# Attention stage: square roots of two batches in a row, three distance buffers, scores two batches ahead

## The reference

```python
P = einsum('btd,ed->bte', Xn, W_in) + b_in      # q, k, v and a gate for each head
sq = q2 + swapaxes(k2, -1, -2) - 2.0 * einsum('bhqd,bhkd->bhqk', Q, K)
dist = sqrt(maximum(sq, 0.0))
W = (1e-4 + dist) ** -2
W = W / (1e-4 + sum(W, axis=-1, keepdims=True))
A = einsum('bhqk,bhkd->bhqd', W, V)
return X + einsum('btd,ed->bte', (G * A) as rows, W_out) + b_out
```

## Time and profile before

| | |
|---|---|
| time, median of 3 runs | 1530.92 us (1530.58 to 1532.08) |
| profiled execution: its time / its span | 1532.71 / 1531.0 us |
| busy of the span: PE, DVE, ACT, POOL | 1312.3, 1277.3, 1095.3, 900.0 us |
| mean granted clock of TensorE | 0.888 |
| attention stage: first distance to last Exp | 832.5 to 1237.3 us |

### The profile page before, as it was taken

One profiled execution on the slowest core, in us unless ns is written; L12 is line 12 of the kernel. 1 busy time (PEld: TensorE's weight loads), 2 busy tenths in 40 slices (PEclk: granted clock), 3 DMA queues, 4 the chain that ended last, 5 costly groups with the idle time before them and its releaser, 6 DMA issues. The chain is left out here.

```text
span 1531.0 us, 21357 instructions
## 1 busy us (share of the span) xinstructions
PE 1312.3 (86%) x6384; PEld 631.9 (41%) x6384; DVE 1277.3 (83%) x2166; ACT 1095.3 (72%) x1578; POOL 900.0 (59%) x1054
## 2 busy tenths in 40 slices
PE   4688888888887699999997788878788669999998
PEld 3344444444443244444443233333333334444443
DVE  2799999999999978788886788888888558888885
ACT  4677777777777446666653899999999956656664
POOL 4988888989887746566665332322222016656665
PEclk8899999999999899999998677676766679999999
DMA  7113112211211022333220000000000023323331
GB/s 249 56 56 111 55 55 64 101 56 55 96 70 56 0 112 112 151 152 139 110 111 1 1 1 0 0 0 0 0 0 0 1 111 119 119 117 118 141 154 64
DMA packets 27923, 111.54 MB, mean 73 GB/s; under 512 B 4049, under 2 KB 9570, under 8 KB 19426
## 3 DMA queue, kind: packets, MB, share of 16 engines
q1 hardware_dynamic: 27010, 110.21, 19.2%
q10 hardware_dynamic: 864, 0.74, 0.2%
HBM read 108.06 MB, written 2.88 MB: 72 GB/s over the span
## 5 line engine op out<-in xcount | busy, mean ns | idle before, releaser
L1042 POOL TENSOR_TENSOR e_h_lo<-e_h,e_h_hi 128x512 f16<-128x512 f32 x272 | 314.9, 1159 | 247.6 <-ACT e_h_hi L1124 235.1
L275 POOL TENSOR_TENSOR m_h<-m_b_sb,m_dx 128x512 f32<-128x512 f32 x256 | 345.7, 1377 | 51.6 <-POOLq L67 40.1
L521 ACT ACTIVATE m_decay<-m_delta,mw_a_log 128x255 f32<-128x255 f32 x448 | 185.3, 461 | 117.3 <-DVEq L695 117.1
L690 DVE TENSOR_TENSOR_SCAN m_h<-m_decay,m_h 128x1024 f32<-128x1024 f32 x112 | 255.9, 2285 | 13.5 <-DVEq L60 7.7
L391 PE MATMUL m_y_ps<-m_hc,ident 128*128 128x512 f32 x512 | 260.7, 635 | 0.0
L1119 ACT ACTIVATE e_g<-e_g 128x512 f32<-128x512 f32 x256 | 148.9, 582 | 126.0 <-PE e_g L1064 124.3
L1124 ACT ACTIVATE e_h_hi<-e_h 128x512 f16<-128x512 f32 x272 | 169.8, 624 | 82.4 <-DVE e_h L1175 80.3
L1621 DVE TENSOR_SCALAR a_d<-a_s 128x512 f32<-128x512 f32 x256 | 170.4, 687 | 55.6 <-PE a_s L1508 35.9
L1064 PE MATMUL e_g<-ef_x_hi,ew_gate_up 128*128 128x512 f16 x544 | 207.9, 382 | 3.8 <-PEq L103 2.4
L1069 PE MATMUL e_y<-e_h_hi,ew_down 128*128 128x512 f16 x544 | 205.9, 379 | 2.4 <-POOL e_h_lo L1042 2.4
L1064 PE MATMUL e_u<-ef_x_hi,ew_gate_up 128*128 128x512 f16 x544 | 207.9, 382 | 0.0
(11 more groups left out here) (234 smaller groups left out, 2067.1 us busy)
## 6 DMA issues: line engine op xcount, KB each, us to landing
e_c_rest<-mix SPq DMA_DIRECT2D x48, 1024.0 KB, 8.7
m_b_sb<-b_rows SPq DMA_DIRECT2D x64, 512.0 KB, 5.4
ef_c_head<-mix SPq DMA_DIRECT2D x16, 1024.0 KB, 4.6
ew_gate_up<-w_gate_up SPq DMA_DIRECT2D x1, 2176.0 KB, 13.5
out<-x_sb SPq DMA_DIRECT2D x8, 256.0 KB, 2.3
ew_down<-w_down SPq DMA_DIRECT2D x1, 1088.0 KB, 11.7
mw_conv_rows<-w_conv_rows ACTq DMA_DIRECT2D x1, 640.0 KB
mix<-ef_cT SPq DMA_DIRECT2D x16, 32.0 KB, 1.6
```

What stands on the lines that cost most here:

```text
L275: ins = nc.gpsimd.tensor_tensor(h[:, m % 4, :, c], b_sb[:, p, 2 * m:2 * m + 2], dx[:, p, c:c + 1].to_broadcast([P, 2, T]), ALU.mult)
L521: ins = nc.scalar.activation(decay_of(m, p)[:, at + 1:at + T], delta[:, p, c, 1:T], ACT.Exp, scale=neg_a[:, c, 2 * m + n:2 * m + n + 1])
L690: nc.vector.tensor_tensor_scan(flat, decay_of(m, p)[:], flat, 0.0, ALU.mult, ALU.add).then_inc(scan_chain, 1)
L1042: nc.gpsimd.tensor_tensor(h_lo[:, k], h[:, k], h_hi[:, k], ALU.subtract).then_inc(h_lo_ready, 1)
```

## The change

ScalarE no longer alternates between the two tables for each batch. It takes the square roots of batches 1 and 2 in a row, then Ln and Exp of batch 1 and of batch 2, and so on for 3 and 4 up to 13 and 14; batches 0 and 15 are done alone as before. For that the scores run two batches ahead (LEAD = 2): body b makes the distances of batch b+2 and the front of batch b+3, into three buffers in turn. The run of bodies begins with b = -2, and six bodies form a loop. The table load for Ln now waits for the roots by a semaphore of its own.

Steps change their places as well. VectorE: the statistics go from head 14 to ahead of distance 0, `normalise` from head 0 to 3, `read_zT` from 4 to 6, the wait for the kept gate from 7 to 9, `read_qkvg` from 8 to 9, `split_qk` from 12 to 13, `update` from 13 to 14. TensorE: `transpose_z` from head 1 to 5. POOL: the norm from the end of a body to its head. The statistics of batch 1, which the expert stage ahead made, move to body -2.

```diff
--- before.py
+++ after.py
@@ AttentionFront.vector_step
         if e == 8:
             self.read_qkvg(dve, 0, banks)
-        if e == 9:
-            self.statistics(dve, 1)
...
@@ attention_layer
         WEIGH_AT = (13, 14, 15)
+        D_BUFS, LEAD, TURN = 3, 2, 6
...
-        d = sb("d", [P, 2, NH, TT * T])
+        d = sb("d", [P, D_BUFS, NH, TT * T])
...
-        def batches(eng, body, prologue, epilogue):
-            prologue()
-            body(-1, 1, core=False, tail=False)
-            body(0, 0, tail=False)
-            with eng.Fori(0, NB // 2 - 2) as i:
-                body(i * 2 + 1, 1)
-                body(i * 2 + 2, 0)
-            body(NB - 3, 1, further=False)
-            body(NB - 2, 0, further=False, ahead=False)
-            body(NB - 1, 1, further=False, ahead=False, heads=False, last=True)
+        def batches(eng, body, epilogue):
+            def run(b, n):
+                body(b, n % 2, n % D_BUFS, n % 2 == 1, opening=n == -LEAD, core=n >= 0, tail=n >= 1, keeps=-1 <= n < NB - 1,
+                     heads=n < NB - LEAD, ahead=n < NB - LEAD - 1, single=n in (0, NB - 1), last=n == NB - 1)
+
+            for n in range(-LEAD, 1):
+                run(n, n)
+            with eng.Fori(0, (NB - LEAD - 2) // TURN) as i:
+                for n in range(1, TURN + 1):
+                    run(i * TURN + n, n)
+            for n in range(NB - LEAD - 1, NB):
+                run(n, n)
             epilogue()
...
@@ POOL, body
-                if ahead:
-                    front.residual(pool, b + 2)
+                if ahead:
+                    front.norm(pool)
+                    front.residual(pool, b + LEAD + 1)
                 if tail:
                     take(pool, gate_free)
-                if heads:
+                if keeps:
                     keep(1 - p)
                 if ahead:
-                    front.pack(pool, p)
-                if further:
-                    front.norm(pool)
+                    front.pack(pool, 1 - p)
...
@@ TensorE, body
-                        score(h, 1 - p, not core)
+                        score(h, p, opening)
                     if h == 1 and tail:
                         weights.wait(-1)
-                        weigh(HG - 1, 1 - p)
-                    if h == 1 and ahead:
-                        front.transpose_z(pe, t_ps[0])
+                        weigh(HG - 1, 1 - p, (k - 1) % D_BUFS)
                     if h == 4 and tail:
                         transpose_av()
+                    if h == 5 and ahead:
+                        front.transpose_z(pe, t_ps[0])
                     if h == 8 and ahead:
                         front.project(pe, t_ps)
...
@@ ScalarE, body
+                def root(buffer):
+                    for first, n in ((0, 8), (8, 4), (12, 4)):
+                        take(act, d_ready)
+                        nc.scalar.activation(heads_of(buffer, first, n), heads_of(buffer, first, n), ACT.Sqrt).then_inc(root_chain, 1)
...
-                for first, n in ((0, 8), (8, 4), (12, 4)):
-                    take(act, d_ready)
-                    nc.scalar.activation(heads_of(first, n), heads_of(first, n), ACT.Sqrt).then_inc(act_chain, 1)
-                nc.scalar.preload_act_table_set("natural_log_exp_and_others")
+                if single or paired:
+                    root(k)
+                    if not single:
+                        root((k + 1) % D_BUFS)
+                    act.wait_ge(root_chain, 3 if single else 6)
+                    act.sem_inc(root_chain, -3 if single else -6)
+                    nc.scalar.preload_act_table_set("natural_log_exp_and_others")
                 for half in range(2):
-                    act.wait_ge(act_chain, 1 + 2 * half)
...
@@ VectorE, body
                 for h in range(NH):
+                    if h == 0 and ahead:
+                        front.statistics(dve, b + LEAD + 1)
                     if heads:
-                        distance(h, 1 - p)
-                    if h == 0 and ahead:
-                        front.normalise(dve, b + 2)
+                        distance(h, (k + LEAD) % D_BUFS)
...
-                    if h == 4 and ahead:
+                    if h == 3 and ahead:
+                        front.normalise(dve, b + LEAD + 1)
+                    if h == 6 and ahead:
                         front.read_zT(dve, t_ps[0])
                     if h == 6 and tail:
                         norm_and_gate(1 - p)
-                    if h == 7 and core:
+                    if h == 9 and keeps:
                         take(dve, gate_ready)
-                    if h == 8 and ahead:
-                        front.read_qkvg(dve, p, t_ps)
+                    if h == 9 and ahead:
+                        front.read_qkvg(dve, 1 - p, t_ps)
                     if h == 10 and tail:
                         read_oT()
-                    if h == 12 and ahead:
-                        front.split_qk(dve, p)
-                    if h == 13 and tail:
+                    if h == 13 and ahead:
+                        front.split_qk(dve, 1 - p)
+                    if h == 14 and tail:
                         update(b - 1)
-                    if h == 14 and further:
-                        front.statistics(dve, b + 3)
...
                     if h == 15 and ahead:
-                        front.read_qkT(dve, p, t_ps)
+                        front.read_qkT(dve, 1 - p, t_ps)
```

More of the change, by code:

```diff
@@ L1477, in keep, with body @@
                 nc.gpsimd.tensor_scalar(gate[:, p], qkvg[:, p, :, 3 * W:4 * W], 1.0, 1.0, ALU.mult, ALU.mult).then_inc(gate_ready, 1)
-            def prologue():
-                front.norm(pool)
-            def body(b, p, core=True, tail=True, heads=True, ahead=True, further=True, last=False):
+            def body(b, p, k, paired, opening, core, tail, keeps, heads, ahead, single, last):
                 if last:
@@ L1572, in body @@
                             weights.wait(g, not tail)
-                            weigh(g, p)
+                            weigh(g, p, k)
                 if heads:
-                    scores_read.end(not core, False)
+                    scores_read.end(opening, False)
                 if core:
-                    weights.end(not tail, not heads)
+                    weights.end(not tail, last)
             def epilogue():
                 weights.wait(HG - 1)
-                weigh(HG - 1, 1)
+                weigh(HG - 1, (NB - 1) % 2, (NB - 1) % D_BUFS)
                 transpose_av()
@@ L1674, in body @@
                         read_av(0)
-                    if h == 2 and tail:
                         read_av(1)
-                    if h == 4 and ahead:
+                    if h == 3 and ahead:
+                        front.normalise(dve, b + LEAD + 1)
+                    if h == 6 and ahead:
                         front.read_zT(dve, t_ps[0])
@@ L1708, in epilogue @@
                 update(NB - 1)
-            batches(dve, body, lambda: None, epilogue)
+            batches(dve, body, epilogue)
 def program(nc, x, w, out, mix, b_rows):
```

31 lines of the change are left out of this document (15 added, 16 removed).

## The result

The changed kernel takes 1554.16 us (median of 4 runs, 1552.46 to 1558.92) against 1531.47 (1530.58 to 1532.08): 1.0154 times the time before, 95% interval 1.0129 to 1.0179. It is slower by 22.7 us, where +12 was forecast. Its runs scatter by 6 us, those of before by 1.5.

The account below looks back on a forecast made before the run. The VectorE and TensorE loop was to replace ScalarE as bound: a start of 901.5, 11 bodies of 24.4 and the tail put the last Exp 12.1 us later, 1530.9 + 12.1 = 1543 us; range 1525 to 1551, forecast's own 1535 to 1548.

Parts of the forecast that it names:

- What bounds: Attention stage: ScalarE bounds at 24.36 us a batch; the VectorE and TensorE loop, about 23.1, is next, about 1.2 behind.
- Part 1, the loads: ScalarE's table loads: 14 fewer, worth 18 us; with a 0.15 wait a pair takes 46.1, a batch 23.05.
- Part 2, the start: First bodies: ScalarE waits for batch 2's distances before batch 1's Ln; batch 2 ends 10.9 us later.
- Part 3 (b): VectorE, end of distance 6 to start of distance 10: readings no longer cover the projection; 6.05 becomes 7.65, +1.6 us.
- Rival 1: ScalarE stays the bound, bodies at or under 23.05 us, about 22 with the projection at full clock; 1525 us; chance 0.17.
- F: Length of a body in the attention stage, forecast at 24.4 us; the difference in time is 11 x F - 256.3.
- Part 3 (a) and (c): Body's start to the end of distance 6, -0.15 us; and from distance 10 on, -0.56 or +0.15.
- (c): Rest of the body from distance 10, 10.3 us before: -0.56 if VectorE is late there, +0.15 if score 15 is late.
- two sums: Body lengths worked out step by step from bodies 1 and 2 of before: 23.9 and 24.9 us, middle 24.4.
- Part 4, the end: From body 12's start at 1169.9 through the last pair and batch 15 alone: last Exp at 1249.4, +12.1 us.
- Rival 3: TensorE's longer waits keep weighing and qk transposes at half clock; bodies 25.0 to 25.3, +19 to +22, 1551 us; chance 0.14.

Follow-up runs that it names:

- e1: Changed kernel with the kept-gate wait and the readings of q, k, v, g put back ahead of distance 9 (head 8); 1529.39 us, ratio 0.9977.
- e2: Kernel before, with only the readings of q, k, v, g moved from behind distance 8 to behind distance 9; 1547.26 us, ratio 1.0107.
- e13: e1 with every batch done singly on ScalarE, 32 table loads; 1529.35 us, ratio 0.9990.
- e11: Changed kernel with two extra unused matmuls of 256 columns behind each of scores 2, 3, 5, 6 and 7; 1533.33 us, ratio 1.0017.
- e4: Changed kernel with every batch done singly on ScalarE, 32 table loads; 1548.09 us, ratio 1.0108.
- e7: Changed kernel with six extra unused matmuls of 256 columns behind score 10; 1548.08 us, ratio 1.0117.
- e14: e7 with its bodies written out instead of looped; 1544.85 us, ratio 1.0097.
- e8: e1 with two extra unused matmuls of 256 columns behind each of scores 2, 3, 5, 6 and 7; 1529.07 us, ratio 0.9988.
- e5: Changed kernel with its bodies written out instead of looped; 1541.74 us, ratio 1.0072.
- e9: e1 with its bodies written out instead of looped; 1525.35 us, ratio 0.9964.
- e10: e8 with its bodies written out and two extra unused matmuls behind scores 10 and 11 as well; 1533.41 us, ratio 1.0006.
- e3: Changed kernel's pairs, three buffers and lead of two, with every step at its head of before and bodies written out; 1536.38 us, ratio 1.0032.

## Why the prediction was right and wrong

The direction, and the mechanism that carries it, were right. Step by step:

- **What bounds.** Right. A batch on ScalarE takes longer than the loop of VectorE and TensorE, and with the change that loop took its place as the bound. e1, e2 and e13 show it: with ScalarE bound or nearly so, 1529; with the loop at 25.4 or more, 1547 and more, pairs or no pairs. But the lead was 24.36 - 23.57 = 0.8 us over the first five bodies, not 1.2.
- **Part 1, the loads.** Right: 18 in the stage, the wait ahead of the load 0.10 (0.15 was taken), and a pair takes 46.1 (e1, from the load at 927.16 to that at 975.42, less a wait of 2.20). In the looped kernels the net worth is nothing that can be told from zero (e13 against e1), since what they win is lost at the start and to the loop. The Trainium skill counts 2.66 us a switch ("ScalarE: Activation LUTs", What ACT_TABLE_LOAD costs); the rows do not agree, a switch costs 1.29 to 1.30 in them.
- **Part 2, the start.** Too dear by 3: body 1 starts at 898.05, not 901.5; the cost is 7.8, not 10.9. The three bodies took 21.6, 22.0 and 22.9 (22.7, 22.7 and 23.5 were taken): the wait for score 9 came in them too, 2.4 to 3.0 us, but most other waits of the first bodies of before went.
- **Part 3 (b).** Right: stretch (2) was to be 7.65 - 0.35 = 7.3 and is 7.18, and distance 9 waits 1.57 (1.55). That this wait hangs on the projection at half clock is shown by e11. Rival 1 had put F at about 22 for that case; it is 23.48 there, since (3) is 10.6.
- **Part 3 (a) and (c), the step that failed.** The length of a body, F, was put at 24.4 and is 25.41. In the stretches of the table the prediction's two sums are on average 7.2 + 7.3 + 9.9 = 24.4; the trace has 7.49 + 7.18 + 10.73. Two terms were too small. The first is the model: bodies 1 and 2 of before, 23.0 and 23.3 us, are the two shortest; the first five average 23.57, because in two of them (3 and 5) the transposes of av run at half clock and (1) is 8.0 instead of 6.9. That is 0.4 us. The second is (c), the rest of the body behind distance 10: it was taken as shorter by 0.56 or longer by 0.15, so 0.2 shorter on average, and it is 0.6 longer than in the first five bodies of before (10.73 against 10.15). That is 0.8 us, and it comes with more of the weighing and of the transposes of q and k at half clock, as bodies 9 and 10 show. The other two stretches give 0.2 back. Over 11 bodies the 1.01 us are +11.1 us; body 1 starts 3.4 earlier than forecast, and the tail is 0.3 longer: 12.1 + 8.0 = 20.1, what the last Exp shows.
- **Part 4, the end.** Right: body 12 starts at 1177.57 and the last Exp ends 79.85 later; 79.5 was worked out. e4 shows that this tail is a price of pairs by itself, about one batch of Ln and Exp (14.5 us).
- **Range.** Its upper end, 1551, was too low by 3 us for the median of 1554.2. The difference of the two profiled executions, +20.0, put on the median of before gives 1551. The rest is scatter: the prediction took a profiled execution as 1.8 above the median, as before, and here it is 1.4 below, with runs up to 1558.9. The range had no term for bodies that differ between executions.
- **Rival 3.** It had the size, 25.0 to 25.3, with 0.14. What it said of the weighing and of the transposes of q and k came true in part: they are at half clock in about half of the bodies. Its reason, that the longer waits of TensorE do it, is neither shown nor refuted, since e7 and e14 left the long wait as it was. The same holds for the warning against gaps that the Trainium skill gives ("TensorE: Matmul & The Clock Gate", Why this matters for your kernels): the page speaks of longer gaps than this one, and no run here tests it. That thin work ahead of the projection goes with half clock in it, and more work there with full clock, is shown by e8 and e11.

What stays open is what decides which bodies meet half clock in the weighing, and so the cause of some 0.8 of the 1.0 us by which F was off. It differs between executions of one kernel (e14: 1539.6 to 1552.6), changes with the loop's turn (e5, e9) and settles into patterns good (e5, 9.6) or bad (e10, 11.4). No run here sets it at will.

## What to carry to other kernels

When two engines hand work to each other in a written order, look at what each long instruction of the one is covered by on the other; moving a reader behind the next hand-over took away that cover and cost 25 us, while the edit that was meant, 18 us of table loads, was worth nothing that shows in the looped kernels and some 4 us at best (e9 against e13). Before removing work from the bound engine, measure how far away the next bound is, here 0.8 us of 24.4, and take its length from all bodies with their clock, not from the shortest two. A lead of one more stage is paid at the start, and pairing is paid again at the end.

## What the runs showed that I had not expected

- Ten matmuls of 256 columns without use in a body bring the matmuls of the projection from 1061 to 593 ns, and make the changed kernel 21 us faster (e11).
- The turn of the loop of six bodies costs VectorE 2.06 us once, but writing the bodies out took 12 us off the changed kernel and 4 off e1 (three runs of e1 were within 1 us of it all the same); the kernel before, bound by ScalarE, did not react (1531.3).
- Bodies that repeat do so at 23.9 us in e3, e5 and e10, three kernels with different work in a body; in e2 they repeat in fours, 25.1, 25.8, 25.2 and 26.3.
- Fillers must be looked up in the trace: those of e7 and e14 stood in a wait of 0.78 us, not in the one of 1.74 for which they were meant.
